# Second cross attention: one DMA transpose for two heads instead of one, and eight buffers for rounded weights instead of four

## The reference

```python
q = fq_sym((x @ Wq + bq) * scale)            # 16 heads of 16 features, all 1024 tokens in one sequence
k = fq_sym(cond @ Wk + bk); v = fq_sym(cond @ Wv + bv, over tokens)
attn = softmax(einsum('bhqd,bhkd->bhqk', q, k))     # 1024 x 1024 for each head
attn = fq_unsigned(attn)                     # round(attn * 255 / rowmax) * rowmax / 255
out = einsum('bhqk,bhkd->bhqd', attn, v) @ Wp + bp
```

## Time and profile before

| what | value |
|---|---|
| median of the runs | 1005.2 us |
| the profiled execution | 1008.87 us, of which the span from the first to the last instruction is 1007.1 us |
| busy time in the span | TensorE 911.9 us (91%), VectorE 668.3 (66%), ScalarE 405.3 (40%), GpSimd 343.2 (34%) |
| transposes | 128 issues, from 350.5 us on |
| attention core | from 346.3 us to about 536.6 us, some 19% of the span |
| chain that ended last, largest line | DMA hT<-hT, the transposes, 10% of the span |

### The profile page before, as it was taken

How to read it: one execution, slowest core, us unless ns; L and a number is a source line. 1 busy time by engine, 2 the same in 40 slices (tenths; PEclk the granted TensorE clock), 3 DMA queues, 4 the chain that set the end, 5 groups by cost and what they waited for, 6 DMA issues and landing times.

```text
span 1007.1 us, 17047 instructions
## 1 busy us (share of the span) xinstructions
PE 911.9 (91%) x5954; PEld 545.8 (54%) x5954; DVE 668.3 (66%) x1331; ACT 405.3 (40%) x683; POOL 343.2 (34%) x365
## 2 busy tenths in 40 slices
PE   7898899999998688889997897989899999999997
PEld 4466665443666444444455454555796658754443
DVE  4987755442569988889994969654112502589998
ACT  3343331310027787788881635631134355210000
POOL 4232203010035476777772621005104557200002
PEclk9997877999999755555557998979899999789999
DMA  9200003000000099999993016056314234000001
GB/s 297 30 1 1 1 1 100 0 1 0 1 1 1 6 180 178 182 180 189 191 184 82 1 37 174 13 138 155 120 48 142 69 95 135 2 0 0 0 0 42
DMA packets 189451, 74.96 MB, mean 74 GB/s; under 512 B 152737, under 2 KB 187196, under 8 KB 189388
## 3 DMA queue, kind: packets, MB, share of 16 engines
q1 hardware_dynamic: 187852, 69.93, 32.5%
q0 software_dynamic: 1536, 4.20, 1.3%
HBM read 33.20 MB, written 7.34 MB: 40 GB/s over the span
## 4 chain that ended last, share of the span: by engine, by line
PE 59%; DVE 16%; DMA 11%; POOL 5%; issue 4%; ACT 4%; SPq 0%; DVEq 0%; ACTq 0%; POOLq 0%
DMA hT<-hT 10%; PE psum L1986 10%; PE psum L446 6%; POOL hT L1048 4%; PE psum L483 3%; PE psum L1543 3%; PE psum L596 2%; PE psum L612 2%; PE psum L450 2%; PE psum L1232 2%; PE psum L426 2%; PE psum L1825 2%; PE psum L337 2%; PE psum L604 1%; PE psum L1786 1%
## 5 line engine op out<-in xcount | busy, mean ns | idle before, releaser
L1112 DVE TENSOR_REDUCE am<-psum 128x1024 f32 (+1 forms) x128 | 154.9, 1222 | 20.1 <-PE psum L958 16.7
L1021 ACT ACTIVATE arena<-psum,am 128x1024 f32<-128x1024 f32 x128 | 142.5, 1113 | 31.0 <-POOL hT L1048 19.8
L1048 POOL TENSOR_SCALAR hT<-arena 128x1024 f16<-128x1024 f32 x128 | 133.9, 1046 | 61.8 <-DMA hT<-hT 32.4
L958 PE MATMUL psum<-arena 96*128 96x512 bf16 x256 | 130.1, 612 | 16.6 <-ACT arena L1021 12.4
L320 POOL TENSOR_TENSOR rstd<-ve,neg_half 128x1 f32<-128x1 f32 x64 | 39.3, 618 | 221.6 <-DVE ve L310 221.3
L1986 PE MATMUL psum<-arena,cT 128*128 x512 | 112.8, 384 | 1.5 <-DVE xn L2044 1.5
L2044 DVE SCALAR_TENSOR_TENSOR xn<-psum,small,xn 128x256 f32<-128x256 f32 x248 | 103.9, 477 | 3.3 <-PE psum L1986 0.2
L1986 PEld LDWEIGHTS psum<-arena,cT 128*128 128x128 f16 x512 | 50.5, 99 | 63.5 <-issue 2.2
L969 PEld LDWEIGHTS psum<-arena,hT 128*128 128x128 f16 x512 | 51.5, 113 | 50.5 <-DMA hT<-hT 24.5
L969 PE MATMUL psum<-arena,hT 128*128 128x16 f16 x512 | 58.6, 185 | 9.1 <-DMA hT<-hT 8.6
L970 PEld LDWEIGHTS psum<-arena,m 128*128 128x128 f16 x512 | 49.4, 114 | 29.9 <-issue 29.6
(11 more groups left out here) (342 smaller groups left out, 1817.2 us busy)
## 6 DMA issues: line engine op xcount, KB each, us to landing
hT<-in_L_ffn_expert_masks SPq DMA_DIRECT2D x32, 256.0 KB, 2.9
arena<-in_L_ffn_w_gate SPq DMA_DIRECT2D x2, 1408.0 KB
arena<-in_L_ffn_w_up SPq DMA_DIRECT2D x2, 1408.0 KB
arena<-in_L_ffn_w_down SPq DMA_DIRECT2D x2, 1408.0 KB
moe_in<-xT SPq DMA_DIRECT2D x2, 1024.0 KB, 6.8
hT<-hT SPq DMA_TRANSPOSE x128, 3.3
hT<-moe_in SPq DMA_DIRECT2D x4, 512.0 KB, 5.5
moe_out<-arena SPq DMA_DIRECT2D x16, 128.0 KB, 1.7
```

What stands on the lines that cost most here:

```text
L958: mm = pe.matmul(psum[:, score_banks(c), :][:, g, :], QT[0:SPLIT, c % H, bass.ds(row_tile(j, c) * P, P)], KT[0:SPLIT, c % H, g * HALF:(g + ...
L1021: act.activation(PE1[:, c % 2, :], psum[:, score_banks(c), :].rearrange("p a b -> p (a b)"), ACT.Exp, bias=am[:, bass.ds(n, 1)], accum_out ...
L1048: pool.tensor_scalar(Y1[:, n % Y_SLOTS, :], PE1[:, n % 2, :], 255.0, 1024.0, ALU.mult, ALU.add)\
L1112: dve.tensor_reduce(am[:, bass.ds(n, 1)], psum[:, score_banks(c), :], AX.XY, ALU.max, negate=True)\
```

## The change

SyncE waits for the rounded weights of two steps and issues one transpose of 128 x 2048 elements (512 KB) for both; there are 64 issues. The rounded weights get eight buffers in four pairs: two where they were, one new in the arena, and one over the start of the arena, which the earlier part of the stage no longer needs. GpSimd now waits for the transpose of step n - 8. The eight buffers for the transposed tiles are the same, used as four pairs; a pair is issued once the value products of both its former steps are done. One semaphore stands for a pair, so the value product of an even step waits until the weights of the step after it have been made, and the transpose of both has landed. `LAG_V` stays 7.

```diff
+        y_homes = [hT[:, 4, :], hT[:, 5, :], a.tile([T]), Arena(arena).tile([T])]
-        PT_SLOTS, Y_SLOTS = 8, 4
+        PT_SLOTS, Y_SLOTS = 8, 8
-        Y1 = hT[:, 4:6, :].rearrange("p a n -> p (a n)").bitcast(FP16).rearrange("p (s n) -> p s n", s=Y_SLOTS)
+        Y1 = [home.bitcast(FP16)[:, i * T:(i + 1) * T] for home in y_homes for i in range(2)]
@@ def turned(h)
-            return sig(f"pt1_slot{h % PT_SLOTS}_landed")
+            return sig(f"pt1_pair{h % PT_SLOTS // 2}_landed")
@@ def xa1_pool(pool)
-                pool.tensor_scalar(Y1[:, n % Y_SLOTS, :], PE1[:, n % 2, :], 255.0, 1024.0, ALU.mult, ALU.add)\
+                pool.tensor_scalar(Y1[n % Y_SLOTS], PE1[:, n % 2, :], 255.0, 1024.0, ALU.mult, ALU.add)\
@@ def turns1(sp)
-            for n in range(NS):
-                wait_step(sp, "y1_ready", n)
-                wait_step(sp, "v1_done", n - PT_SLOTS)
-                sp.dma_start_transpose(PT1[:, n % PT_SLOTS, :, :], Y1[:, n % Y_SLOTS, :]).then_inc(turned(n % H), 16)
+            for n in range(0, NS, 2):
+                wait_step(sp, "y1_ready", n + 1)
+                wait_step(sp, "v1_done", n + 1 - PT_SLOTS)
+                at = n % PT_SLOTS
+                sp.dma_start_transpose(PT1[:, at:at + 2, :, :].rearrange("p s k q -> p (s k) q"),
+                                       y_homes[n % Y_SLOTS // 2].bitcast(FP16)).then_inc(turned(n % H), 16)
```

## The result

The changed kernel is slower. Side by side it takes 1016.71 us against 1006.03 us for the kernel before, medians of twelve runs each; the ratio is 1.0086 with a 95% interval of 1.0058 to 1.0115, which on 1006 us is 8.7 us, with an interval of 5.8 to 11.6, where 7.1 was forecast. The profiled execution took 1017.8 us (span 1016.1), against 1008.87 (1007.1) before.

The account below looks back on a forecast made before the run. SyncE's issuing of transposes, 1.374 us a step, was taken to bound the kernel. Loop 1.8, fetches 4.4 and end 0.9 us made 7.1, added to the median 1005.2: 1012.3, rounded to 1012; range 1000 to 1026.

Parts of the forecast that it names:

- What bound before: Attention core: SyncE's issuing of transposes sets the pace, 1.374 us a step; GpSimd's 30.1 us of waits are mostly backlog.
- Halving the issues: SyncE's queue: 1.33 us a step at the long end, no longer binding; alone at best 5.6 us gained, at VectorE's pace.
- The buffers: GpSimd's eight buffers for rounded weights: its waits for transposes go, but were backlog, so nothing is booked.
- The landing: Transpose of 512 KB in the core: lands after 4.55 us instead of 3.3, with 5.85 us as upper end.
- The late start: Rival, chance 0.20: the longer issue also delays the start of the transfer in the core; 1022 us, in full 1033.
- The loop: Core, closed path from scores through rounding and landing to next scores: 11.1 us for eight steps, 1.388 each, binds; 1.8 us worse.
- The fetches: Instruction fetches in the core delay landings without slack: nine at 1.3 us instead of 0.8, 4.4 us worse.
- The end: After the core's last rounding: landing 4.55 us instead of 3.95, and two value products instead of one; 0.9 us worse.

Follow-up runs that it names:

- the second trace: The changed kernel itself, run again on another chip beside the kernel before: ratio 1.007, 187.6 us for the 127 steps.

## Why the prediction was right, and where its sizes were off

**What bound before.** Right. With eight buffers and a longer lag the single transposes still went out at 1.38 us each, and nothing was gained.

**Halving the issues.** Right that SyncE would not bind after, in the quiet steps; where the fetches run, some issues last 3 us and more, and with a lag of nine SyncE's queue is unbroken there. That an issue's length does not mirror the state of the DMA engines, as the prediction read it from the first two, does not hold then. The median length of one issue, taken at its long end of twice 1.288, was 1.94 to 2.00 us.

**The buffers.** Booked at nothing and measured at nothing (0.9992); that they are needed by the pairs was not weighed, and costs 41 us where they are missing.

**The landing.** Forecast 4.55 us, measured 4.5. The late start does not happen, as the first pair shows: its issue, and then GB/s in slices of 0.1 us from 354.1:

```profile
354.11 1.89 SPq L1151 DMA_TRANSPOSE hT<-hT  x1
...
GB/s 0 0 0 0 0 0 0 0 0 0 0 0 10 136 215 233 207 230 202 212 215 200 210 220 215 218 220 207 225 215 212 228 212 207 164 120 146 174 205 264
```

Data flow 1.3 us after the start, as in the earlier trace rows, while the issue lasts 1.89. The Trainium skill's fixed cost plus bytes (DMA: Bandwidth & Descriptors, "Anatomy of one DMA"), fitted there to DMAs that GpSimd issues, would have made the landing an estimated 3.9 us and the change faster; the trace decides against it for these transposes.

**The loop.** The mechanism held, and its size nearly: in the quiet steps the issues' pace of 1.374 was measured at 1.378, and the loop's 1.388 at 1.395 and 1.398; moving the lag moved the time both ways. The term of 1.8 us is then (1.395 - 1.378) x 127 = 2.2, and 2.5 in the second trace. VectorE's own pace was taken too slow: 1.30 with a lag of eight and more, not 1.33.

**The fetches.** Forecast 4.4 us worse, nine fetches at 1.3 us instead of 0.8. What the 127 steps take above the quiet pace was before 181.8 - 175.0 = 6.8 us for nine, 0.8 each; after, 185.8 - 177.2 = 8.6 for eight (the ninth comes with the last rounding), 1.1 each; in the second trace 187.6 - 177.5 = 10.1 for nine, 1.1 each. So the 0.8 was right, the 1.3 too high, and the fetches cost 1.8 to 3.3 us more than before. How much is the loop's and how much the fetches' depends on the steps that are called quiet: by the steps 83 to 119, at 1.376 before and 1.383 after, the loop would get 0.9 us and the fetches 3.1. Only the sum of both, 4.0 us and 5.8 in the second trace, is firm.

That slack absorbs them is shown in part. By the paces of the two stretches a fetch costs 0.8 us with a lag of six ((1.691 - 1.604) x 79 / 9), 0.95 to 1.06 with seven, 0.95 with eight, 0.4 with nine and 0.3 with ten. With two steps more it costs less, but one step more does not change it, and six, where there is no slack, is below seven. That may be because the transfers then have idle time between them; no run tried it.

**The end.** Forecast 0.9 us; from the start of the last rounding to that of the last product 544.4 - 537.8 = 6.6 us against 536.6 - 531.2 = 5.4, 1.2 us, and 0.7 in the second trace.

```profile
537.75 1.05 POOL arena L1049
538.81 0.47 SPq L1151
539.37 4.33 DMA hT<-arena
```

**The sum.** In the profiles the core, from the first rounding to the last product, takes 192.5 us against 187.2: 5.3 us of the 9.0 between the spans. In the second trace it takes 193.7, 6.5 more, where the runs beside it said 7.1. Of the 9.0 another 2.5 lie ahead of the core: its first rounding begins at 351.9 instead of 349.4, in work that the change does not touch. I don't put that down to the change, since the same start varied from 342.1 to 354.7 among the kernels above, and was 345.5 in the second trace of the changed one. Whether the rest of the measured 8.7 us is more than such scatter stays open; the interval's lower end, 5.8, is close to the core's 5.3. The forecast of 7.1 comes as near as it does partly by luck: its term for the fetches was 1 to 3 us too high, and up to 3 us of the measured time lie outside the core, where it has no term.

## What to carry to other kernels

A larger transfer saves issues and makes every landing later, so ask which closed path the landing lies on and how many steps that path spans; if the pace is near the path's length divided by its steps, lengthen the lag together with the transfer. To name the paces, compare steps that no other traffic disturbs: one fetch near the end made the old pace look as slow as the new one. Here the same change loses 0.9% at a lag of seven and gains 1 to 1.7% at nine or ten. A long wait in the list of waits is no gain in store when the engine named only stands behind a full queue: with more buffers the wait moved to TensorE and the time stayed.

## What the runs showed of the hardware

With a lag of seven the median DMA transpose of 512 KB occupies SyncE for 1.94 to 2.00 us, one of 256 KB for 1.29. An estimate from these is a fixed part of about 0.6 us and 0.7 us for each 256 KB. It is no constant of a transpose: single issues of 512 KB lasted from 1.64 us to 3.5, and with a lag of nine the median is 2.3:

```profile
L1151 SPq DMA_TRANSPOSE hT<-hT x32: 1793/2282/3560, 350.1 to 512.4; - x32
```

Of either size, the first transfer of the core begins 1.3 us after the start of its issue (the earlier trace rows and the row of GB/s above). The landing of 512 KB grows with the load too, from 4.5 us with a lag of seven to 4.7 with nine and 4.8 with ten.

A DMA share of 1.01 in the earlier trace rows was read as full engines, and wrongly. With a lag of nine the same engines moved more in the same time, 203 GB/s at a share of 1.12, where the undisturbed stretch before had 188 at 1.03 (columns as in the earlier trace rows):

```profile
461.00:520.00 59.00, 54.48 (x634) 29.96 (x632) 52.85 (x63) 51.12 (x86) 46.05 (x44) 0.50 1.12 203
```
